# Causal attention on one core: score products in F32R on halves of the partitions, two heads at a time

## The chip, the cores and the metric

The kernel runs on one core of a Trainium2 chip. TensorE (PE) multiplies, VectorE (DVE), ScalarE (ACT) and GpSimd (POOL) work beside it, and SyncE (SP) issues most transfers. The metric is the device time of one execution in microseconds: median 2697.65 us of three runs (2695.6 to 2702.26).

## The reference, cut to what matters

Two layers, each attention times a gated mixture of experts. The change lies in the first attention and in what prepares it; x is 2 x 2048 x 256, with 16 heads of 16.

```python
xn = _layernorm(x)
q = (xn @ Wq.T).reshape(B, S, H, hd).transpose(0, 2, 1, 3)      # k and v alike
scores = einsum('bhcd,bhsd->bhcs', qi, k) * hd ** -0.5          # a block of 64 queries
scores = where(kpos[None, :] <= qpos[:, None], scores, finfo.min)
out = einsum('bhcs,bhsd->bhcd', softmax(scores), v)
s = out @ Wo.T
g = silu(experts(xn))                                           # top 1 of 8, capacity T / 8
x = x + s * g
# layer 2: windows of 128 with a look back, rotary q and k, 16 heads of 64; experts top 2 of 8
```

## The kernel before, in words

The stages follow each other: stage_project (layer norm, q, k, v, router), stage_attention, stage_experts, stage_join, stage_windows. T = 4096 rows are worked in chunks of CH = 512; P = 128, TC = 4 tiles a chunk, QC = 4 chunks a batch entry, KT = 16 key tiles.

**stage_project.** Per chunk, q and k come as four products psq[m] in PSUM. Each is written as three bf16 parts whose sum is the float32 value: ACT takes the first (L425), DVE the rest (L367), ACT the second part (L430), DVE the third (L372). SP stores all three to qk_parts in DRAM (L308). PE's next products wait for the rest (L476).

**stage_attention** goes through eight groups: four groups of GH = 4 heads (`groups`, L630), each for both batch entries u. q and k are loaded six times each, in pairs of parts, to stand on 96 partitions (parts_q, parts_k, L587), so that one bf16 matmul with 96 rows gives a product of nearly float32 precision. Three more rows of kb are ones and three of qa hold minus the query's maximum in three parts (MR = 99), so the score product comes out with the maximum subtracted.

Each group has two streams, woven by attention_steps (L493) into one list that all engines follow in order:
- "A" (maxima, a_step L715): 128 queries by up to 512 keys of one head into one of three single banks (RING = 3), DVE reduces the bank to a maximum (L859) and frees it. On the diagonal a second matmul adds -1e30 to future keys (L724). PE waits for the bank's own last user, three turns back (L720). When a chunk of queries is complete ("M"), DVE splits the negated maxima (L866 to L870), PE turns them ("MT", L731), DVE copies them out (L876) and SP writes them as rows of qa (L691).
- "S" (scores, L774): 128 keys by up to 512 queries of one head into one bank of a pair; the mask is added by a matmul on the diagonal (L777). After two heads ACT takes the exponentials of both banks (L836) into one of four slots of probs. "PV" (L792): for four heads, v with a column of ones times the probabilities, in float32, each head on its own 32 output partitions, accumulated over key tiles; it stands one key tile behind the scores. At a chunk's end "COPY" (ACT, L844) and "O" (four turns through a ring bank, L802, and the division, L906 and L909).

The A stream runs half a group ahead of the scores (LEAD = 0.5): its first half for group 0 is the head (L736), and each group carries the second half of its own maxima and the first of the next. GpSimd meanwhile fills constant parts (L655 to L660), clears expert_in (L665) and scatters 32 tiles into it (L668). SP loads the next group's q, k and v (L677 to L679) ahead of the rows of maxima that follow in its queue.

## Time and profile before

| | us |
|---|---|
| median of 3 runs | 2697.65 |
| lowest, highest | 2695.6, 2702.26 |
| span of the profiled execution, its own time from first to last instruction | 2692.8 |
| PE, DVE, ACT, POOL busy | 2451.3, 1846.2, 1406.8, 815.1 |

The profile is of one execution; no time but its span is given for it. Start and duration in the timeline are in us, the trace's PE rows are matmuls and its PEld rows weight loads. Matmuls are pipelined, so successive starts tell their rate and not their duration. The projections end at about 132 us, the first attention at 1157 us.

### The profile page before, as it was taken

Reading aid. Unit: us, or ns where it says so; the run is one execution under the profiler, and the core shown is the slowest. Engines: PE = TensorE matmul, PEld = TensorE weight load, DVE = VectorE, ACT = ScalarE, POOL = GpSimd, SP = SyncE. Lnnn points to the kernel's source line nnn. Section 1 sums busy time; section 2 is a strip of 40 time slices with the busy share of each in tenths; the row PEclk is TensorE's granted clock in tenths of the full one; section 3 lists DMA queues with packets and bytes.
Section 4 is the critical chain, followed back from the end, with each engine's and each line's share of the span. In section 5 each row is a group of like instructions: output and inputs, shape, how many; then the busy total and the mean of one; then the engine's idle time right before and its main releaser. Section 6 shows DMA issues by size and latency. Waiting matters only on the chain. (4 is left out here: it accounts for less than half of the span.)

```text
span 2692.8 us, 51134 instructions
## 1 busy us (share of the span) xinstructions
PE 2451.3 (91%) x16420; PEld 1589.0 (59%) x16420; DVE 1846.2 (69%) x3682; ACT 1406.8 (52%) x2776; POOL 815.1 (30%) x647
## 2 busy tenths in 40 slices
PE   5648999999999999969977599999999999999999
PEld 4512333333333333358866477777777777777777
DVE  7757877877787777424438476777667767766776
ACT  3404655656565566755634255555555555555554
POOL 1070000000000000014425355554455555444553
PEclk9858999999999999989988699999999999999999
DMA  4574041321404040033257000000000000000000
GB/s 135 191 170 65 5 62 26 41 52 16 61 6 62 6 60 5 7 127 133 102 177 241 18 13 12 11 13 13 13 13 13 9 11 13 13 13 13 13 9 9
DMA packets 189865, 132.85 MB, mean 49 GB/s; under 512 B 99857, under 2 KB 177687, under 8 KB 189712
## 3 DMA queue, kind: packets, MB, share of 16 engines
q1 hardware_dynamic: 160048, 100.06, 15.4%
q10 hardware_dynamic: 24160, 14.16, 2.2%
q0 software_dynamic: 5504, 16.69, 1.7%
q8 instruction: 83, 1.36, 0.2%
q14 instruction: 70, 0.57, 0.1%
HBM read 84.43 MB, written 46.14 MB: 48 GB/s over the span
## 5 line engine op out<-in xcount | busy, mean ns | idle before, releaser
L859 DVE TENSOR_REDUCE a_best<-a_ring 128x1 f32<-128x512 f32 (+3 forms) x1280 | 700.9, 604 | 214.0 <-PE a_ring L721 123.0
L836 ACT ACTIVATE a_probs<-a_pss 128x1024 f32<-128x1024 f32 (+3 forms) x640 | 554.0, 895 | 452.6 <-PE a_pss L777 228.7
L721 PE MATMUL a_ring<-a_kb,a_qa 96*128 96x512 bf16 (+3 forms) x1280 | 453.0, 365 | 67.2 <-DVE a_best L859 32.3
L774 PE MATMUL a_pss<-a_qa,a_kb 99*128 99x512 bf16 (+3 forms) x1280 | 433.9, 353 | 15.6 <-issue 7.2
L1771 ACT ACTIVATE w_probs<-w_pss,w_top 128x256 f32<-128x256 f32 x512 | 239.0, 476 | 379.7 <-DVE w_top L1859 365.0
L1606 POOL TENSOR_TENSOR w_probs<-w_probs,w_inv 128x512 f32<-128x512 f32 x256 | 301.0, 1176 | 395.7 <-DVE w_inv L1865 386.3
L962 POOL TENSOR_TENSOR e_w_r<-e_w,e_w_r 128x1024 fp32r<-128x1024 f32 x28 | 67.0, 2402 | 1032.7 <-ACT e_w_r L1035 1032.7
L1629 PE MATMUL w_psw<-wqkv,w_xr 128*128 128x512 f32 x1152 | 301.5, 398 | 11.6 <-POOL w_xr L1563 11.6
L774 PEld LDWEIGHTS a_pss<-a_qa,a_kb 99*128 99x128 bf16 x1280 | 123.5, 98 | 302.6 <-ACT a_probs L836 224.5
L792 PE MATMUL a_acc<-a_probs,a_vg 128*32 128x512 f32 (+3 forms) x2560 | 299.9, 541 | 0.1
L1669 PE MATMUL w_pss<-w_kd,w_qt 128*128 128x256 f32 x1536 | 278.4, 310 | 0.0
L1859 DVE TENSOR_REDUCE w_top<-w_pss 128x2 f32<-128x512 f32 x256 | 176.8, 691 | 141.5 <-PE w_pss L1669 140.7
L721 PEld LDWEIGHTS a_ring<-a_kb,a_qa 96*128 96x128 bf16 x1280 | 126.4, 99 | 223.9 <-DVE a_best L859 128.6
L1629 PEld LDWEIGHTS w_psw<-wqkv,w_xr 128*128 128x128 f32 x1152 | 205.6, 190 | 47.6 <-POOL w_xr L1563 12.1
L1669 PEld LDWEIGHTS w_pss<-w_kd,w_qt 128*128 128x128 f32 x1536 | 222.0, 195 | 4.1
L1629 PE MATMUL w_psw<-we,w_xr 128*128 128x512 f32 x768 | 204.2, 401 | 0.0
L1710 PE MATMUL w_pso<-w_pt,w_v 128*64 128x128 f32 x2048 | 168.3, 285 | 0.1
L1689 PE MATMUL w_pst<-identity,w_probs 128*128 128x128 f32 x1024 | 155.7, 275 | 0.0
L1629 PEld LDWEIGHTS w_psw<-we,w_xr 128*128 128x128 f32 x768 | 134.9, 188 | 22.9 <-issue 0.2
L1689 PEld LDWEIGHTS w_pst<-identity,w_probs 128*128 128x128 f32 x1024 | 123.6, 140 | 31.2 <-issue 5.7
L1882 DVE SCALAR_TENSOR_TENSOR w_y<-w_psw,coef,w_y 128x256 f32<-128x256 f32 x224 | 108.3, 484 | 42.4 <-PE w_psw L1629 23.2
L1710 PEld LDWEIGHTS w_pso<-w_pt,w_v 128*64 128x64 f32 x2048 | 106.5, 136 | 49.6 <-issue 49.1
(223 smaller groups left out, 3771.2 us busy)
## 6 DMA issues: line engine op xcount, KB each, us to landing
e_w<-in_w SPq DMA_DIRECT2D x16, 1024.0 KB, 7.9
qk_parts<-p_parts SPq DMA_DIRECT2D x32, 384.0 KB, 3.7
a_qa<-qk_parts SPq DMA_DIRECT2D x192, 64.0 KB, 2.5
a_kb<-qk_parts SPq DMA_DIRECT2D x42, 256.0 KB, 9.5
p_xin<-in_x SPq DMA_DIRECT2D x8, 512.0 KB, 5.4
v_rows<-p_vout SPq DMA_DIRECT2D x8, 512.0 KB, 5.1
a_vg<-v_rows SPq DMA_DIRECT2D x32, 128.0 KB, 9.1
expert_in<-zero POOLq DMA_DIRECT2D x16, 256.0 KB, 8.3
```

Of the source, the lines that this page charges most:

```text
L721: ins = pe.matmul(bank[:, 0:keys], qa[u][0:QR, i // TC, h, (i % TC) * P:(i % TC + 1) * P], kb[u][0:QR, h, k * CH:k * CH + keys], start=Tru ...
L774: ins = pe.matmul(pss[idx % 2][:, e, lo:CH], kb[u][0:MR, h, j * P:(j + 1) * P], qa[u][0:MR, c, h, lo:CH], start=True, stop=(j < TC * c))
L792: ins = pe.matmul(acc[32 * h:32 * h + 32, lo:CH], vg[u][:, j, h, :], probs[:, 2 * (pv % 2) + h // 2, h % 2, lo:CH], start=(j == 0), stop=( ...
L836: act.activation(probs[:, idx % 4, :, lo:CH], pss[idx % 2][:, :, lo:CH], ACT.Exp).then_inc(exp_done, 1)
L859: vec.tensor_reduce(best[:, i // TC, h * TC + i % TC, k:k + 1], bank[:, 0:keys], X, ALU.max).then_inc(ring_taken, 1)
L1606: pool.tensor_tensor(probs[:, p % 4, :, :], probs[:, p % 4, :, :], inv[:, :, p:p + 1].to_broadcast([P, 2, 2 * P]), ALU.mult).then_inc(p_re ...
L1629: ins = pe.matmul(psw[bank][:, :], xr[a][:, src, k, :], moving(b, k), start=(m == 0), stop=(m == len(pairs) - 1))
L1669: ins = pe.matmul(scores, qt[a][:, p, :], keys[b][:, p, :, :], start=False, stop=(a, b) == PARTS[-1])
L1689: ins = pe.transpose(pst[r % 2][:, 2 * e + role, :], probs[:, p % 4, e, role * P:(role + 1) * P], keep["identity"][:, :])
L1710: ins = pe.matmul(pso[e * DH:(e + 1) * DH, p % 4, :], v[(u + 1 + role) % 2][:, h * DH:(h + 1) * DH], pt[:, p % 2, 2 * e + role, :], start= ...
L1771: ins = act.activation(probs[:, p % 4, e, :], pss[p % 2][:, e, :], ACT.Exp, bias=top[:, e, p:p + 1], accum_out=rows[:, e, p:p + 1])
L1859: vec.tensor_reduce(top[:, :, p], pss[p % 2][:, :, :], X, ALU.max, negate=True).then_inc(top_ready, 1)
```

## The change: what it does

q and k are split into two F32R parts instead of three bf16 parts. The three products of parts (high-high, high-low, low-high) take 48 rows, with two rows for the maxima 50. The even head of a pair stands on partitions 0 to 49, the odd one on 64 to 113. "A" and "S" are steps of two heads: an A step fills two ring banks and waits for ring_taken up to the first item of the pair before; an S step fills both banks of a pair. The mask of the maxima becomes four bf16 matmuls of 64 rows, two for each half. The scores get no mask: the exponentials of the diagonal block are cleared by GpSimd (affine_select, behind a one-column add), and PV waits on future_cleared there. The rows of ones come by four transfers from a constant instead of a memset on GpSimd; neg_parts is split in three steps instead of five; the rows of maxima go out in four transfers of float32 instead of three of bf16. The number of q and k loads stays 24 and 6, and so do their bytes; a store of parts is 512 KB instead of 384.

```diff
-QR = 6 * HD
-MR = QR + 3
+QR = 3 * HD
+MR = QR + 2
+HALF = P // 2
...
+            for half, low_base in ((0, -HALF), (1, 0)):
+                for part, base in ((slice(0, P), low_base), (slice(0, HALF), HALF * half)):
+                    ch.link(pool.memset(keep["turn_halves"][part, half, :], 0.0))
+                    ch.link(pool.affine_select(out=keep["turn_halves"][part, half, :], in_=keep["turn_halves"][part, half, :],
+                                               compare_op=ALU.not_equal, fill=1.0, base=base, pattern=[[-1, P]],
+                                               channel_multiplier=1))
+                    ch.link(pool.affine_select(out=keep["qk_halves"][part, half, :], in_=keep["zero16"][part, :],
+                                               compare_op=ALU.is_ge, fill=NEG, base=base, pattern=[[-1, P]],
+                                               channel_multiplier=1))
+            ch.link(pool.memset(keep["ones32"][:, :], 1.0))
...
-        rest = st.sb("rest", [P, 4, CH])
-        parts = st.sb("parts", [P, 4, 3, CH], BF16)
+        parts = st.sb("parts", [P, 4, 2, CH], F32R)
...
-                def rest_of(m):
-
-                    vec.wait_ge(first_part, 4 * c + m + 1)
-                    vec.scalar_tensor_tensor(out=rest[:, m, :], in0=psq[m][:, :], scalar=HD ** -0.5 if m < 2 else 1.0,
-                                             in1=parts[:, m, 0, :], op0=ALU.mult, op1=ALU.subtract).then_inc(rest_ready, 1)
-
-                def third(m):
-                    vec.wait_ge(second_part, 4 * c + m + 1)
-                    vec.tensor_tensor(parts[:, m, 2, :], rest[:, m, :], parts[:, m, 1, :], ALU.subtract
-                                      ).then_inc(parts_ready, 1)
-
                 for m in range(4):
-                    rest_of(m)
-                for m in range(4):
-                    third(m)
+                    vec.wait_ge(high_part, 4 * c + m + 1)
+                    vec.scalar_tensor_tensor(out=parts[:, m, 1, :], in0=psq[m][:, :], scalar=HD ** -0.5 if m < 2 else 1.0,
+                                             in1=parts[:, m, 0, :].bitcast(F32), op0=ALU.mult, op1=ALU.subtract
+                                             ).then_inc(parts_ready, 1)
...
-        for h in range(GH):
+        for g in range(GH // 2):
             for i in range(TC * c, TC * c + TC):
                 for k in range(c + 1):
-                    maxima.append((h, i, k))
+                    maxima.append((g, i, k))
...
-            for h in range(GH):
-                steps.append(("S", c, j, h))
+            for g in range(GH // 2):
+                steps.append(("S", c, j, g))
...
-    parts_q, parts_k = (0, 0, 1, 1, 0, 2), (0, 1, 0, 1, 2, 0)
-    n_loads = len(parts_q) * QC + len(parts_k)
+    parts_q, parts_k = (0, 0, 1), (0, 1, 0)
+    q_loads, k_loads = 2 * len(parts_q), 2 * len(parts_k)
+    n_loads = q_loads * QC + k_loads
+    M = GH * TC
+    M_LANDED = 4 * 16
...
-        qa = [st.sb(f"qa{u}", [MR, QC, GH, CH], BF16) for u in range(2)]
-        kb = [st.sb(f"kb{u}", [MR, GH, S], BF16) for u in range(2)]
+        qa = [st.sb(f"qa{u}", [P, QC, GH // 2, CH], F32R) for u in range(2)]
+        kb = [st.sb(f"kb{u}", [P, GH // 2, S], F32R) for u in range(2)]
...
-            for u in range(2):
-                pool.memset(kb[u][QR:MR, :, :], 1.0).then_inc(ones_set, 1)
...
+            for g, i, u, order in groups(pool):
+                idx = 0
+                for s in order:
+                    if s[0] == "S":
+                        _, c, j, hp = s
+                        if j >= TC * c:
+                            lo = (j - TC * c) * P
+                            pool.wait_ge(exp_done, primed + g * n_s + idx + 1)
+                            pool.tensor_tensor(spare[:, idx % GH:idx % GH + 1], keep["zero"][:, 0:1], keep["zero"][:, 0:1], ALU.add)
+                            block_probs = probs[:, idx % GH, :, lo:lo + P]
+                            pool.affine_select(out=block_probs, in_=block_probs, compare_op=ALU.is_ge, fill=0.0, base=0,
+                                               pattern=[[0, 2], [1, P]], channel_multiplier=-1).then_inc(future_cleared, 1)
+                        idx += 1
...
+            def masked(bank, e, x, stop):
+
+                return pe.matmul(bank, keep["turn_halves"][half(e, HALF), x, :], keep["qk_halves"][half(e, HALF), x, :],
+                                 start=False, stop=stop)
+
+            def a_step(u, s, r, banks):
+                _, dg, g, i, k = s
                 keys = min(CH, (i + 1) * P - k * CH)
                 diagonal = k == i // TC
 
-                wait(pe, ring_taken, r + 1 - RING)
-                ins = pe.matmul(bank[:, 0:keys], qa[u][0:QR, i // TC, h, (i % TC) * P:(i % TC + 1) * P],
-                                kb[u][0:QR, h, k * CH:k * CH + keys], start=True, stop=not diagonal)
+                wait(pe, ring_taken, r + 2 - RING)
+                for e in range(2):
+                    ins = pe.matmul(banks[e][:, 0:keys], qa[u][half(e, QR), i // TC, g, (i % TC) * P:(i % TC + 1) * P],
+                                    kb[u][half(e, QR), g, k * CH:k * CH + keys], start=True, stop=not diagonal)
+                    if not diagonal:
+                        ins.then_inc(ring_full, 1)
                 if diagonal:
-                    ins = pe.matmul(bank[:, keys - P:keys], keep["identity16"][:, :], keep["mask_qk"][:, :],
-                                    start=False, stop=True)
-                ins.then_inc(ring_full, 1)
+                    for x in range(2):
+                        for e in range(2):
+                            ins = masked(banks[e][:, keys - P:keys], e, x, x == 1)
+                            if x == 1:
+                                ins.then_inc(ring_full, 1)
...
+            for u in range(2):
+                for e in range(2):
+                    at = HALF * e + QR
+                    sp.dma_start(kb[u][at:at + 2, :, :].bitcast(F32).rearrange("o g (k n) -> o (g k) n", n=CH),
+                                 keep["ones32"][0:2, :].unsqueeze(1).to_broadcast([2, GH // 2 * S // CH, CH])
+                                 ).then_inc(ones_set, 16)
...
-                        if e == 0:
-
-                            pe.wait_ge(exp_done, primed + g * n_s + max(idx - 1, 0))
-                        ins = pe.matmul(pss[idx % 2][:, e, lo:CH], kb[u][0:MR, h, j * P:(j + 1) * P],
-                                        qa[u][0:MR, c, h, lo:CH], start=True, stop=(j < TC * c))
-                        if j >= TC * c:
-                            ins = pe.matmul(pss[idx % 2][:, e, lo:lo + P], keep["identity16"][:, :],
-                                            keep["mask_kq"][:, :], start=False, stop=True)
-                        if e == 1:
-                            ins.then_inc(s_ready, 1)
-                            idx += 1
+                        if j == 0 and hp == 0:
+
+                            pe.wait_ge(m_landed[c], M_LANDED * (g + 1))
+
+                        pe.wait_ge(exp_done, primed + g * n_s + max(idx - 1, 0))
+                        for e in range(2):
+                            ins = pe.matmul(pss[idx % 2][:, e, lo:CH], kb[u][half(e, MR), hp, j * P:(j + 1) * P],
+                                            qa[u][half(e, MR), c, hp, lo:CH], start=True, stop=True)
+                        ins.then_inc(s_ready, 1)
+                        idx += 1
                     elif s[0] == "PV":
                         _, c, j = s
                         lo = max(0, j - TC * c) * P
-                        pe.wait_ge(exp_done, primed + g * n_s + 2 * pv + 2)
+                        if j < TC * c:
+                            pe.wait_ge(exp_done, primed + g * n_s + GH // 2 * (pv + 1))
+                        else:
+                            pe.wait_ge(future_cleared, g * n_diagonal + GH // 2 * (j + 1))
...
-                vec.wait_ge(ring_full, r + 1)
-                vec.tensor_reduce(best[:, i // TC, h * TC + i % TC, k:k + 1], bank[:, 0:keys], X, ALU.max
-                                  ).then_inc(ring_taken, 1)
+                for e in range(2):
+                    vec.wait_ge(ring_full, r + e + 1)
+                    vec.tensor_reduce(best[:, i // TC, e, g * TC + i % TC, k:k + 1], banks[e][:, 0:keys], X, ALU.max
+                                      ).then_inc(ring_taken, 1)
...
                 ch.link(vec.tensor_copy(neg_parts[:, 0, :], neg[:, :]))
-                ch.link(vec.tensor_tensor(neg_rest[:, :], neg[:, :], neg_parts[:, 0, :], ALU.subtract))
-                ch.link(vec.tensor_copy(neg_parts[:, 1, :], neg_rest[:, :]))
-                vec.tensor_tensor(neg_parts[:, 2, :], neg_rest[:, :], neg_parts[:, 1, :], ALU.subtract).then_inc(m_split, 1)
+                vec.tensor_tensor(neg_parts[:, 1, :], neg[:, :], neg_parts[:, 0, :].bitcast(F32), ALU.subtract
+                                  ).then_inc(m_split, 1)
```

In stage_project ACT's second(m) (L428) is gone too, and PE's L476 waits for parts_ready. qk_parts becomes [2, 2, D, T] in float32.

## Rows read from the trace of the kernel before

**Rows 1.** Page, part 1: busy us (share of the span) xinstructions.
```profile
PE 2451.3 (91%) x16420; PEld 1589.0 (59%) x16420; DVE 1846.2 (69%) x3682; ACT 1406.8 (52%) x2776; POOL 815.1 (30%) x647
```
**Rows 2.** Timeline, main part's first score, last division: start, us, engine, line, op.
```profile
223.60 0.63 PE L774 MATMUL a_pss<-a_qa,a_kb 99*128 99x512 bf16 x1
...
1156.40 0.42 DVE L909 TENSOR_TENSOR a_oout<-a_ring,a_inv 128x256 f32<-128x256 f32 x1
```
**Rows 3.** Windows: stretch, length, engines' busy us (instructions), PEclk, DMA share, GB/s.
```profile
43.00:55.00 12.00, 10.45 (x61) 9.00 (x60) 11.47 (x39) 7.65 (x19) 1.04 (x1) 1.00 0.72 232
151.00:183.00 32.00, 26.42 (x95) 8.74 (x95) 29.21 (x68) 0.00 (x0) 18.98 (x27) 0.50 0.79 218
185.00:214.00 29.00, 4.90 (x12) 0.89 (x10) 5.13 (x8) 0.00 (x0) 19.62 (x20) 0.50 0.30 112
280.00:320.00 40.00, 38.63 (x271) 14.63 (x263) 32.41 (x79) 23.69 (x27) 0.00 (x0) 1.00 0.03 6
```
**Rows 4.** Waits, 140 to 1100 us: us in total, times, longest.
```profile
DVE a_best L859 <- PE a_ring L721: 122.1, 170, 4.1
```
**Rows 5.** Timeline, weight loads of two PV bursts three turns apart.
```profile
265.01 0.16 PEld L792 LDWEIGHTS a_acc<-a_probs,a_vg 128*32 128x32 f32 x8 [0.43 <-issue]
...
273.68 0.16 PEld L792 LDWEIGHTS a_acc<-a_probs,a_vg 128*32 128x32 f32 x8 [0.16 <-issue]
```
**Rows 6.** Timeline, maxima, scores and one PV burst.
```profile
258.91 1.28 DVE L859 TENSOR_REDUCE a_best<-a_ring 128x1 f32<-128x512 f32 x2
...
260.24 0.10 PEld L721 LDWEIGHTS a_ring<-a_kb,a_qa 96*128 96x128 bf16 x1 [0.32 <-DVE a_best L859]
260.24 0.39 PE L721 MATMUL a_ring<-a_kb,a_qa 96*128 96x512 bf16 x1
...
260.47 0.38 PE L774 MATMUL a_pss<-a_qa,a_kb 99*128 99x512 bf16 x1
...
260.84 0.39 PE L721 MATMUL a_ring<-a_kb,a_qa 96*128 96x512 bf16 x1
261.16 0.16 PEld L792 LDWEIGHTS a_acc<-a_probs,a_vg 128*32 128x32 f32 x8 [0.23 <-issue]
...
262.16 0.10 PEld L774 LDWEIGHTS a_pss<-a_qa,a_kb 99*128 99x128 bf16 x1 [0.84 <-ACT a_probs L836]
```
**Rows 7.** F32R in the second layer: durations in ns, min/median/max, and timeline.
```profile
L1629 PEld LDWEIGHTS w_psw<-we,w_xr x5: 188/188/192, 1707.4 to 1708.2; 128*128 128x128 f32 x5
L1629 PE MATMUL w_psw<-we,w_xr x4: 393/395/478, 1707.4 to 1708.2; 128*128 128x512 f32 x4
...
1707.44 1.18 PE L1629 MATMUL w_psw<-we,w_xr 128*128 128x512 f32 x4
...
1704.52 1.55 PE L1629 MATMUL w_psw<-we,w_xr 128*128 128x512 f32 x6
```
**Rows 8.** Groups by shape, 245 to 1110 us: busy us, mean ns, idle before.
```profile
L859 DVE TENSOR_REDUCE a_best<-a_ring 128x1 f32<-128x128 f32 x115 | 32.4, 282 | 8.1 <-PE a_ring L724 8.1
```
**Rows 9.** Timeline, a group's end.
```profile
581.49 0.58 ACT L844 COPY a_sums<-a_acc 128x512 f32<-128x512 f32 x1 [0.55 <-PE a_acc L792]
...
582.20 0.65 PE L802 MATMUL a_ring<-identity,a_sums 128*128 128x128 f32 x4 [0.78 <-ACT a_sums L844]
```
**Rows 10.** GpSimd: a select at the start, a two-operand pass in the second layer.
```profile
L117 POOL TENSOR_SCALAR_AFFINE_SELECT identity<-identity 128x128 f32<-128x128 f32 x1 | 0.3, 283 | 0.2 <-POOL identity L116 0.2
...
L1606 POOL TENSOR_TENSOR w_probs<-w_probs,w_inv 128x512 f32<-128x512 f32 x256 | 301.0, 1176 | 395.7 <-DVE w_inv L1865 386.3
```
**Rows 11.** Groups of the projections, 43 to 91 us.
```profile
L425 ACT ACTIVATE p_parts<-p_psq 128x512 bf16<-128x512 f32 x17 | 10.2, 597 | 15.7 <-DMA qk_parts<-p_parts 15.7
L372 DVE TENSOR_TENSOR p_parts<-p_rest,p_parts 128x512 bf16<-128x512 f32 x16 | 10.0, 686 | 0.2 <-ACT p_parts L430 0.2
```
**Rows 12.** Timeline, GpSimd's memset of ones and SP's loads for group 1.
```profile
137.02 13.79 POOL L660 MEMSET a_kb<- 3x8192 bf16 x2
...
182.57 33.66 SPq L641 DMA_DIRECT2D a_qa<-qk_parts  x15
```

More of the change, by code:

```diff
@@ L882, in _ @@
                 if s[0] == "A":
-                    take(s, r, ring[r % RING])
+                    take(s, r, [ring[(r + e) % RING] for e in range(2)])
                 elif s[0] == "M":
@@ L894, in _ @@
                     if s[0] == "A":
-                        take(s, at, bank)
+                        take(s, at, [bank_of(u, r + e) for e in range(2)])
                     elif s[0] == "M":
```

159 lines of the change are left out of this document (82 added, 77 removed).

## The prediction

> **What bounds the kernel now.** The page first: PE is busy for 91% of the span [rows 1]. Then the windows: the change lies in the projections (before 132 us) and in the first attention, which runs from 151 to 1156 us; its main part, eight head groups, takes 932.8 us from the first score product to the last division [rows 2], 116.6 us a group. In the middle of it, at a granted clock of 1.00, PE is busy 38.6 of 40 us, DVE 32.4, ACT 23.7 [rows 3]: PE's in-order stream is the bound, with DVE's maxima close behind. The waits say how close: DVE waited 122 us for score products for the maxima [rows 4], in gaps of under a microsecond. Between bursts of the value product (PV), one turn with full widths (8 score matmuls, 4 reductions, 2 exponentials, PV) takes 2.89 us, a third of the way from the first row to the last of [rows 5]. In PE's own terms: a bf16 matmul of 512 columns follows the one before after 0.22 us, and from PV's first weight load to the next 128-column load is 1.00 us, 0.10 us after the stream before it ended [rows 6]: 8 x 0.22 + 1.00 + 0.10 = 2.86.
>
> **What the change does to PE's work.** A score product of one head (96 or 99 rows, bf16) becomes one of 48 or 50 rows in F32R on one half of the partitions; two heads go together. F32R streams 512 columns in (1.55 - 0.40)/5 = 0.23 us [rows 7], no slower than bf16. Whether two halves of rows run at once no row shows. Bounds: 0.23 us a pair if they do, 0.47 if not. I take 0.23, since PV puts four column strips side by side: eight float32 matmuls of 512 columns in 1.00 us, which one after another would need at least 8 x 0.22 [rows 6]. With it PE's stream of a full turn falls from 2.86 to 4 x 0.23 + 1.10 = 2.0 us, and PE is no longer the bound. The Trainium skill (TensorEngine Tiling, Tiling Modes) says that tiles of 64 x 128 work independently and load and multiply in parallel; by it the sum below stands, against it the rival of 2820 us holds; the trace agrees for columns, 1.00 us for eight.
>
> **What is late next: the ring of three banks.** DVE itself could do a pair of full reductions in 2 x 0.60 (two in 1.28 us, the last of them 0.68) [rows 6]. But a pair of maxima now takes two banks at once, and its matmuls wait until the first bank of the pair before is free. So the reductions form a chain: reduction 0.68; from its end to the weight load 0.05 (reductions end at 260.19, load at 260.24) [rows 6]; weight load and product L; to DVE 0.04. For bf16 L is 0.39 [rows 6]. An F32R weight load takes 188 ns against 98, and after a wait the product took 478 ns instead of 395, 0.03 us after the load's start [rows 7]: L = 0.50. Another matmul was streaming then, so L may be as little as 0.40; I take 0.50, the row's own value. Period of a full pair: 0.68 + 0.05 + 0.50 + 0.04 = 1.27 us. Narrow ones: a reduction of 128 columns takes 282 ns [rows 8], so 133 ns a step up to 512; L falls by 0.05 a step; the diagonal's mask is now two more pairs of 128 columns, 0.11 us. That makes 1.38, 1.20, 1.02 and 0.82 us for diagonal pairs of 512, 384, 256 and 128. A group has 48 full pairs and 8 of each diagonal width: 61.0 + 35.4 = 96.4 us.
>
> **What crosses this chain.** PE keeps program order: score pair, maxima pair, score pair, maxima pair, PV. Between two maxima without PV everything fits under 1.27 us. With PV in between, PE needs: load 0.11, pair 0.23, gap 0.10, PV 1.00, score load 0.11 and pair 0.23, less the 0.11 of the next load behind it: 1.67 us, 0.40 over the chain; after a narrow pair 0.53 to 0.79. A full turn becomes 1.27 + 1.67 = 2.94 us, against 2.89 now: the halved PE work is given back whole. By the order of the steps there are 26 such full-width crossings a group, 18 after full pairs and 8 after narrow ones: 18 x 0.40 + 8 x 0.61 = 12.1.
> - Single-bank turns: after one (4 of the maxima, 3 outputs inside the group) the next pair must wait for both banks of the pair before: 0.60 each after maxima, 0.65 after outputs, 4.4 in all; the maxima's split holds DVE 0.65 us, four times, 2.6. The split loses two of its five steps, which is in the 0.65.
> - Stretches with narrow scores and few maxima, where PE waits for exponentials: 1.5 + 1.0, estimated from the narrow turns of now. The group's end: after the last maxima pair its stream and two narrow PVs end at 2.6 us; the last PV waits for its exponentials and their clear, to 3.4, and takes 0.3; copy 0.6, four turns 0.65 [rows 9], a score pair: 5.4 us, 4.1 over a chain period, 0.7 of it the clear.
> Sum 96.4 + 12.1 + 7.0 + 6.6 = 122.1; about 1.5 of it coincides (splits that fall beside a PV): 120.6 us a group against 116.6, +4.0. The last group has maxima in only half: 7.5 x 4.0 = +30 us. With L = 0.40 the 52 periods without PV lose 0.10 each: 115.4, -9 us. If the two row halves load weights one after the other, 28 crossings gain up to 0.2: +5.6 a group, +42.
>
> **The clears.** 32 a group: a one-column add and a select over 128 x 256. Select over 128 elements 0.28 us, a GpSimd two-operand pass over 512 elements 1.18 [rows 10]: between 0.3 and 0.6 for 256, I take 0.45, and 0.1 for the add. GpSimd is idle in the main part [rows 3]. PV stands a whole turn (2.9 us) behind its exponentials, so 1.1 us for two is hidden, except at the group's end (counted). The mask matmuls that go from the scores (64 x 0.06 us) save PE time that no longer bounds.
>
> **Projections.** DVE is busy 11.5 of 12 us a chunk, PE 10.5 [rows 3]: DVE bounds. Four of its passes of 0.69 us go [rows 11], and ACT's four. PE and its waits are next at about 10.8. Seven chunks by 1.2: -8 us. Bounds: 0, if the stores (512 KB in place of 384 KB each; ACT already waits for them) take over, and -14.
>
> **The head of attention** (151 to 223.5 us) runs at granted clock 0.50, DVE-bound at first, then almost still from 185 to 214 (12 matmuls in 29 us, [rows 3]), while SP issues the next group's loads (182.57, 33.7 us for 15) beside the scatter. The chain at half clock costs 1.5 us for a full pair against 1.2: 43 pairs, +16 us with masks. The 13.8 us memset of ones goes from GpSimd [rows 12], so the scatter ends that much earlier and the still stretch shrinks: -12. Net +4, bounds -20 and +20. The loads keep number and bytes; four small loads of ones come behind them, covered by the head.
>
> **Sum.** The span is 2692.8 us; the median of the runs, 2697.65, is 4.9 above it, and I keep that. 2697.65 + 30 - 8 + 4 = 2724 us.
>
> **Rivals.**
> - Faster: the F32R weight load hides, so L = 0.40, and the head gives back more of its still stretch (0 net instead of +4). Then 2697.65 - 9 - 8 = 2681. It decides at L = 0.42, where the main part breaks even. For it: in steady streams F32R at 256 columns keeps pace; against it: the 478 ns row.
> - Row halves in turn: the full crossing grows by 0.47, the other periods are still the chain's: +13 a group: 2697.65 + 17 x 7.5 - 4 = 2820. Against it stand PV's strips.
> - The clears bound: at 0.6 and 0.1, a GpSimd whose spans are longer under DVE's traffic could pass 1.2 us each; eight in each diagonal are then 10 us, against some 8 us of other work there: +1.5, four times a group: 2724 + 45 = 2769. For it: GpSimd pays 1.18 us for 512 elements [rows 10].
> - The clock: with PE's stream at two thirds, it could stay at 0.50 as in the head, where PE was busy 26 of 32 us and was not granted more [rows 3]. A full turn at 1.2 GHz is some 4.8 us, 60% more: near 3280. Against it: the projections hold 1.00 at 10.5 of 12 us. The Trainium skill (TensorE: Matmul & The Clock Gate, Part 1) calls the throttled state the default that activity releases; the head agrees, 0.50 throughout.
>
> **How the numbers follow.** This kernel's runs tell 0.3% (8 us) from no change. Forecast 0.52 (its own range 2705 to 2750), faster 0.25, clears 0.10, row halves in turn 0.10, clock 0.03. The faster rival lies in part within 0.3% only if the head disappoints. Faster 0.27, same 0.15, slower 0.58. Range: 2668, below the faster rival by the projections' and head's bounds, to 2795, which takes in the clears, or the serial weight loads with the bounds of head and projections.
>
> **What would show it.** Right: in the full turns, pairs of reductions start 1.27 and 1.67 us apart in turn, DVE's idle time before them ends with a maxima matmul, PE is busy clearly less than 38 of 40 us, and the group takes 119 to 122 us. The two matmuls of a pair start within 0.02 us. Wrong: L of 0.40 in the wait-limited pairs; matmuls of a pair 0.23 apart; PV waiting for selects inside a group; a granted clock under 1 in the main part; projections no shorter than now.

## The result, and the profile after

The changed kernel took 2881.5 us, the median of 4 runs (2871.6 to 2894.9), the kernel before 2696.6 us beside it (2693.3 to 2702.3): a ratio of 1.068, 95% interval 1.065 to 1.072. Measured again on another chip it was 1.069 (1.065 to 1.073). The forecast was 2724 us, its range 2668 to 2795: slower was right, the size was not.

The page of the kernel after, part 1 (against [rows 1]), and from part 2 the granted clock of PE in 40 slices, in tenths:

```profile
PE 2495.5 (87%) x16420; PEld 1618.0 (56%) x16420; DVE 1846.4 (64%) x3591; ACT 1390.2 (48%) x2744; POOL 945.0 (33%) x1168
...
PEclk9756788786869687867998769999999999999999
```

The same row of the page of the kernel before:

```profile
PEclk9858999999999999989988699999999999999999
```

This is the first thing to see. Slices 4 to 18 hold the main part before, 4 to 19 after. Before, the clock stands at its upper level (1.00, 2.4 GHz) there; after, it goes back to 0.50 (1.2 GHz) again and again. Two windows give it as one number each: the whole main part, first score product to last division, before (its ends are in [rows 2]):

```profile
223.60:1156.80 933.20, 891.19 (x6176) 337.39 (x6174) 702.83 (x1443) 569.05 (x672) 0.00 (x0) 0.99 0.21 32
```

and windows of the kernel after: a projection chunk; the stretch in the middle of the head in which PE and DVE hardly work, called the still stretch here; the main part, and within it four of 10 us and one of 40 us:

```profile
42.00:54.00 12.00, 11.39 (x74) 10.09 (x72) 10.04 (x35) 5.95 (x18) 1.39 (x2) 1.00 0.81 276
...
172.00:203.00 31.00, 4.05 (x22) 1.94 (x22) 4.82 (x10) 0.00 (x0) 20.75 (x22) 0.50 0.22 90
...
236.80:1343.40 1106.60, 936.38 (x6130) 357.84 (x6128) 716.26 (x1380) 567.65 (x672) 138.97 (x512) 0.79 0.17 26
...
440.00:450.00 10.00, 7.92 (x66) 3.13 (x66) 7.17 (x16) 5.28 (x6) 0.00 (x0) 0.95 0.00 0
450.00:460.00 10.00, 9.42 (x53) 3.49 (x51) 4.76 (x11) 3.18 (x4) 2.19 (x8) 0.50 0.01 3
460.00:470.00 10.00, 9.37 (x61) 4.17 (x61) 5.83 (x14) 4.49 (x7) 2.19 (x8) 0.50 0.00 1
470.00:480.00 10.00, 9.09 (x54) 3.54 (x52) 6.43 (x12) 5.28 (x7) 0.00 (x0) 0.68 0.01 1
...
480.00:520.00 40.00, 31.41 (x257) 11.88 (x255) 30.00 (x58) 22.16 (x26) 4.33 (x16) 1.00 0.03 7
```

The main part grew from 933.2 to 1106.6 us. At clock 1.00 PE is busy 31.4 of 40 us, against 38.6 before [rows 3]: thinned, as forecast. In 440 to 450 us its busy time is 7.9 of 10, and then the clock is 0.50, for 27 us in this case. Over the main part there are 30 such falls with 475 us at 0.50; before there were 2 with 18 us. At 0.50 PE's busy share reads higher (9.4 of 10), because the same instructions take longer: a full engine is here a sign of a slow one.

The timeline of a full turn after, at clock 1.00, compared with [rows 5] and [rows 6]:

```profile
500.82 0.16 PEld L812 LDWEIGHTS a_acc<-a_probs,a_vg 128*32 128x32 f32 x8
500.82 1.07 PE L812 MATMUL a_acc<-a_probs,a_vg 128*32 128x512 f32 x8
...
502.58 2.57 DVE L881 TENSOR_REDUCE a_best<-a_ring 128x1 f32<-128x512 f32 x4 [0.64 <-PE a_ring L738]
503.33 0.19 PEld L738 LDWEIGHTS a_ring<-a_kb,a_qa 48*128 48x128 f32 x2 [0.99 <-DVE a_best L881]
503.33 0.50 PE L738 MATMUL a_ring<-a_kb,a_qa 48*128 48x512 f32 x2 [0.54 <-DVE a_best L881]
503.76 0.16 PEld L812 LDWEIGHTS a_acc<-a_probs,a_vg 128*32 128x32 f32 x8 [0.24 <-issue]
```

From one value product to the next 503.76 - 500.82 = 2.94 us, the forecast's number. The two maxima products of a pair, one on each half of rows, share one start and together last 0.50 us: they run side by side, and L is 0.50. DVE's four reductions stand back to back for 2.57 us, with one gap a turn that ends with the pair behind the value product: 2.94 - 2.57 = 0.37 us between full turns, 0.64 us here, where two reductions of 384 columns stood before it. A full turn at clock 0.50, same kernel:

```profile
260.65 1.93 PE L812 MATMUL a_acc<-a_probs,a_vg 128*32 128x512 f32 x8
...
262.52 0.79 PE L795 MATMUL a_pss<-a_qa,a_kb 50*128 50x512 f32 x2
...
264.52 0.80 PE L738 MATMUL a_ring<-a_kb,a_qa 48*128 48x512 f32 x2 [0.36 <-DVE a_best L881]
265.25 0.20 PEld L812 LDWEIGHTS a_acc<-a_probs,a_vg 128*32 128x32 f32 x8 [0.44 <-issue]
```

265.25 - 260.65 = 4.60 us: the value product takes 1.93 us instead of 1.07, and every full turn that falls into a stretch at 0.50 (a cold one, for short) costs 1.66 us more.

To part the clock from the rest, cut each group into its 40 turns (two exponentials each), take for each turn of the group the shortest time in seven groups, of those free of cold time where there are any, and add them: 115.9 us before, 124.1 after. That is +8.2 us, or 62 us over 7.5 groups (the last group has maxima in only half). The other 112 of the main part's 173 us are then put down to the clock.

This split is not clean, and it gives the clock too little. The 2nd, 3rd, 6th, 7th, 14th and 15th turn of a group are partly cold in all seven groups after, and they hold 4.3 of the 8.2 us; the 34 turns that are seen at full clock give 3.9. Experiment 10 below, which only adds work, has the 6th turn at full clock at 3.87 us (5.24 here) and the 14th at 3.08 (4.47 here). These two alone move 2.8 us a group to the clock: the turns are then +5.4 us a group, some 41 us, and the clock has some 132 us. A check from the other side: in the places seen at both levels, 82 cold turns are together 94 us longer than the median of the others in the same place; the 3rd, 6th, 7th, 14th and 15th turns are together, over seven groups, 43 us above their times in experiment 10. And the four executions of this kernel go with the clock: 2894.9 us with a mean of 0.869 over the span, 2871.6 with 0.879.

| us | before | after | difference | forecast |
|---|---|---|---|---|
| projections, end | 132.3 | 124.2 | -8.1 | -8 |
| loads, to the first maxima product | 18.9 | 19.6 | +0.7 | 0 |
| head | 72.4 | 93.0 | +20.6 | +4 |
| main part, sums of shortest turns | 7.5 x 115.9 | 7.5 x 124.1 | +62 (some 41 at full clock) | +30 |
| main part, the rest: the clock | | | +112 (some 132) | 0 |
| the rest of the span | 1536.0 | 1540.3 | +4 | 0 |

The waits of DVE after, 140 to 1290 us, show where its idle time went (against 122.1 us in [rows 4]), and the rows of GpSimd's clears with PE's wait for them what these cost:

```profile
DVE a_best L881 <- PE a_ring L738: 208.9, 288, 4.1
DVE a_best L881 <- PE a_ring L728: 139.8, 173, 18.0
...
PE a_acc L812 <- POOL a_probs L668: 10.5, 28, 0.6
...
L668 POOL TENSOR_SCALAR_AFFINE_SELECT a_probs<-a_probs 128x256 f32<-128x256 f32 x256 | 104.6, 409 | 0.0
L666 POOL TENSOR_TENSOR a_spare<-zero 128x1 f32<-128x1 f32 x256 | 49.8, 195 | 1002.6 <-ACT a_probs L856 1000.4
```

### The profile page after: what moved, and what is told of

Read it like the earlier page. It is cut to its first block and busy times, and to the rows that moved or that the text cites. A ratio compares the mean times of both kernels' runs of the same rounds, so it can differ in the third digit from the quotient of the medians.

```text
span 2883.7 us, 51101 instructions
## 1 busy us (share of the span) xinstructions
PE 2495.5 (87%) x16420; PEld 1618.0 (56%) x16420; DVE 1846.4 (64%) x3591; ACT 1390.2 (48%) x2744; POOL 945.0 (33%) x1168
## 5 line engine op out<-in xcount | busy, mean ns | idle before, releaser
L881 DVE TENSOR_REDUCE a_best<-a_ring 128x1 f32<-128x512 f32 (+3 forms) x1280 | 721.1, 606 | 381.9 <-PE a_ring L738 209.2
L738 PE MATMUL a_ring<-a_kb,a_qa 48*128 48x512 f32 (+3 forms) x1280 | 329.9, 512 | 221.1 <-DVE a_best L881 190.9
L812 PE MATMUL a_acc<-a_probs,a_vg 128*32 128x512 f32 (+3 forms) x2560 | 376.4, 667 | 10.6 <-POOL a_probs L668 10.5
L666 POOL TENSOR_TENSOR a_spare<-zero 128x1 f32<-128x1 f32 x256 | 49.8, 195 | 1002.6 <-ACT a_probs L856 1000.4
L738 PEld LDWEIGHTS a_ring<-a_kb,a_qa 48*128 48x128 f32 x1280 | 149.5, 230 | 362.9 <-DVE a_best L881 330.0
L795 PE MATMUL a_pss<-a_qa,a_kb 50*128 50x512 f32 (+3 forms) x1280 | 323.7, 513 | 9.4 <-issue 7.1
L795 PEld LDWEIGHTS a_pss<-a_qa,a_kb 50*128 50x128 f32 x1280 | 143.1, 225 | 324.7 <-issue 160.7
## 6 DMA issues: line engine op xcount, KB each, us to landing
expert_in<-zero POOLq DMA_DIRECT2D x16, 256.0 KB, 16.9
```

The lines of the kernel that those rows point to most:

```text
L738: ins = pe.matmul(banks[e][:, 0:keys], qa[u][half(e, QR), i // TC, g, (i % TC) * P:(i % TC + 1) * P], kb[u][half(e, QR), g, k * CH:k * CH ...
L795: ins = pe.matmul(pss[idx % 2][:, e, lo:CH], kb[u][half(e, MR), hp, j * P:(j + 1) * P], qa[u][half(e, MR), c, hp, lo:CH], start=True, stop ...
L812: ins = pe.matmul(acc[32 * h:32 * h + 32, lo:CH], vg[u][:, j, h, :], probs[:, GH // 2 * (pv % 2) + h // 2, h % 2, lo:CH], start=(j == 0), ...
L881: vec.tensor_reduce(best[:, i // TC, e, g * TC + i % TC, k:k + 1], banks[e][:, 0:keys], X, ALU.max).then_inc(ring_taken, 1)
```

## The experiments

Two theories at the start. A: PE's stream, thin after the change, is what lets the granted clock fall, and the fall is most of the loss. B: the turns are longer by their waits and the clock does little. All runs below were timed beside the kernel before; "fills" are products written into a score bank ahead of the scores that overwrite them, which change nothing in the output. The columns: ratio to the kernel before with its interval; a full turn (the 17th of a group); sum of the shortest turns, as above; the main part; time at clock 0.50 in it with the number of falls. Experiments 1 to 4 and 9 to 15 ran on chips where the kernel before takes 2670 to 2673 us, the others where it takes 2695 to 2697. The head is shorter on the former (last section), so experiments of different chips are compared by their main parts; that a main part is the same on both was not measured. All columns but the ratio are of one profiled execution; those of experiments 1 and 9 took 32 and 19 us more than their medians. In most runs two to nine of the 40 turns are partly cold in all seven groups, so differences of two or three us in the group's sum are not read.

| | ratio | full turn | group | main | cold, falls |
|---|---|---|---|---|---|
| before | 1 | 2.96 | 115.9 | 933 | 18, 2 |
| after | 1.068 (1.065 to 1.072) | 2.95 | 124.1 | 1107 | 475, 30 |
| 1 scores doubled | 1.055 (1.049 to 1.062) | 3.17 | 132.3 | 1109 | 290, 24 |
| 2 own-bank waits | 1.040 (1.036 to 1.043) | 2.93 | 119.2 | 1069 | 428, 26 |
| 3 before, pair waits | 1.032 (1.030 to 1.035) | 3.42 | 127.3 | 1015 | 19, 2 |
| 4 no clears | 1.059 (1.055 to 1.062) | 2.94 | 126.3 | 1080 | 423, 31 |
| 5 after again | 1.069 (1.065 to 1.073) | 2.93 | 125.4 | 1099 | 448, 29 |
| 6 fills on all rows | 1.075 (1.073 to 1.078) | 3.26 | 135.4 | 1132 | 166, 18 |
| 7 before, lighter | 1.025 (1.021 to 1.029) | 3.26 | 122.2 | 987 | 107, 16 |
| 8 fills at narrow turns | 1.086 (1.082 to 1.089) | 2.94 | 134.3 | 1163 | 349, 29 |
| 9 bf16 halves | 1.011 (1.008 to 1.014) | 2.74 | 116.2 | 981 | 285, 33 |
| 10 fills in the gap | 1.047 (1.043 to 1.050) | 2.93 | 125.9 | 1038 | 144, 16 |
| 11 value product cut | 1.043 (1.036 to 1.050) | 2.62 | 117.9 | 1045 | 414, 29 |
| 12 both of 2 and 11 | 1.022 (1.018 to 1.026) | 2.60 | 114.7 | 1011 | 364, 27 |
| 13 before, thin | 1.016 (1.013 to 1.020) | 3.05 | 116.8 | 971 | 154, 17 |
| 14 bf16 and both | 0.991 (0.988 to 0.995) | 2.43 | 107.3 | 908 | 171, 18 |
| 15 the same, fills | 0.998 (0.996 to 0.999) | 2.69 | 110.2 | 938 | 110, 12 |
| 16 two bf16 parts | 0.973 (0.971 to 0.975) | 2.42 | 105.9 | 880 | 160, 24 |

**1. The same work twice.**
```diff
-                        for e in range(2):
+                        for e in (0, 1, 0, 1):   # score pair
```


> The changed kernel, with each pair of score matmuls issued twice; the second overwrites the first, so the result is the same and PE has 0.23 us more to do per exponential. Theory A (the clock follows how much PE works; the chain of reductions leaves it idle and it falls to 0.50 in parts of the main part): a full turn at full clock grows from 2.94 to about 3.2 us by the crossing with PV, but the granted clock rises from 0.78 to over 0.9 in the main part, and the time falls from 2882 to about 2780. Theory B (the clock falls for another reason, such as the matmuls' 48 rows, whatever PE's load): the clock stays below 0.8 and the time rises by 60 to 100 us, to about 2960.

2828.5 us. The full turn grows by 0.22 us and the group by 8 us, as expected, or some 61 us in all; yet the main part of the profiled execution, itself 32 us over the median, is no longer than the changed kernel's, since 185 us of cold time go. A is supported, but the clock came only to 0.87 in the main part and the time is 50 us over the expectation. The four executions spread with the clock: 2860.3 us at a mean of 0.909 over the span, 2801.7 at 0.935.

**2. Each half waits for its own bank.**
```diff
-                wait(pe, ring_taken, r + 2 - RING)
                 for e in range(2):
+                    wait(pe, ring_taken, r + e + 1 - RING)
```


> The changed kernel, with each half of a maxima pair waiting for its own bank alone, so that the ring is three deep again; the halves then often run one after the other. Theory A: the chain of reductions is gone, DVE is kept at its own rate, a full turn takes about 2.6 us with PE at 2.5, the clock stays at 1.00 for nearly all of the main part, a group takes 106 to 110 us and the kernel about 2640, faster than the kernel before. Theory B: turns at full clock get shorter but the clock stays near 0.8; about 2800.

2803.7 us. The 2.6 us turn did not come: PE keeps order, and the value product still stands ahead of the next pair. The group's sum is 5 us smaller, 2.1 of them in the 6th turn, which is cold in all groups of the changed kernel and once at full clock here. The head takes 51 us where experiment 1 on the same chip has 67.

**3. The wait alone, in the kernel before.**
```diff
-                wait(pe, ring_taken, r + 1 - RING)
+                wait(pe, ring_taken, r + 2 - maxima_seen[0] % 2 - RING)
+                maxima_seen[0] += 1
```


> The kernel before (bf16, 96 rows), with one edit: every other maxima matmul waits for one bank more, as the first of a pair does in the changed kernel. Theory A: PE is now idle for lack of banks, full turns take about 3.1 us and the granted clock falls below 1.00 in the main part; the time is 2800 to 2900. Theory B: the clock stays at 1.00, and the time is about 2780 by the longer turns alone.

2759.4 us. By A the clock was to fall; it fell no more than in the kernel before, and the time is that of B. So waits for banks alone don't bring the clock down. PE was still busy 912 of 1015 us of the main part, in bf16 on all rows. What was missing for a fall is asked in 7 and 13.

**4. No clears**, and PV waits for the exponentials only (the future keys' probabilities stay in the output).
```diff
-                            block_probs = probs[:, idx % GH, :, lo:lo + P]
-                            pool.affine_select(out=block_probs, ...).then_inc(future_cleared, 1)
...
-                            pe.wait_ge(future_cleared, g * n_diagonal + GH // 2 * (j + 1))
+                            pe.wait_ge(exp_done, primed + g * n_s + GH // 2 * (pv + 1))
```


> The changed kernel without GpSimd's clears and without PV's wait for them: the probabilities of future keys in the diagonal blocks are left in, so the output is not the reference's. My prediction put 1 to 2 us a group on the clears: 10 us, 2870 against 2882. The rival that the clears bound the diagonals says 40 us or more.

2824.2 us, by its ratio 1.0% under experiment 5. Of that the main part has 19 us, and 25 us less of cold time are in it. Full turns are the same. What the clears cost stands at the group's end: its last turn at full clock takes 3.77 us, 4.64 in experiment 5, where the forecast counted 0.7 us for the clear. The sum of the shortest turns is no smaller, since nine of its turns are cold in all seven groups.

**5. The changed kernel again**, on its own chip with 6 to 8.

> The changed kernel itself, so that the experiments have it on their own chip. By its first measurement (1.068 times the kernel before, 2671 us there) about 2853 us, granted clock near 0.87 over the span. In experiment 4 the changed kernel without its clears came to 1.059 times the kernel before: if that difference is real, this one is 0.8 to 1.0% slower than it.

2878.1 us. The first measurement's ratio is confirmed. Its profiled execution is 448 us cold where the first has 475: so much the cold time varies between executions.

**6. Fills on all rows.**
```diff
+                        for t in range(4):
+                            pe.matmul(pss[idx % 2][:, 0, t * P:(t + 1) * P], keep["turn_halves"][:, 0, :],
+                                      keep["qk_halves"][:, 0, :], start=True, stop=True)
```


> Ahead of each pair of score products, at every width, PE does four bf16 products of 128 rows by 128 columns into the same bank, which the score product then overwrites: 0.24 us of work a pair, as the duplicates of experiment 1, but on all rows of the array, and also full size where the scores are narrow. Theory A (the granted clock follows PE's load): the same full turn of 3.17 us, clock 0.87 to 0.92, 2800 to 2830 us. Rival (products on half of the rows count less for the clock): clock 0.95 or more, cold time in the main part under 80 us, and about 2780 us by the longer turns.

2899.9 us, over both expectations. Clock 0.93 in the main part and cold time 166 us, between the two; it also fills narrow turns, so "on all rows" and "more of it" are not parted. The full turn of 3.26 us costs more than the clock gives back.

**7. The kernel of 3 with a thin stream.**
```diff
-                        ins = pe.matmul(pss[idx % 2][:, e, lo:CH], kb[u][0:MR, h, j * P:(j + 1) * P],
-                                        qa[u][0:MR, c, h, lo:CH], start=True, stop=(j < TC * c))
+                        ins = pe.matmul(pss[idx % 2][:, e, lo:lo + P], kb[u][0:MR, h, j * P:(j + 1) * P],
+                                        qa[u][0:MR, c, h, lo:lo + P], start=True, stop=(j < TC * c))
```


> The kernel of experiment 3 (the kernel before with the wait for a second bank at every other maxima product), and every score product cut to its first 128 columns, so that the output is not the reference's: bf16, 96 and 99 rows, no F32R in the attention. PE's stream of a full turn falls from 2.86 to about 2.2 us, in turns of 2.8 to 3.1 us: the share that the changed kernel has. Theory A (load alone): the granted clock falls to 0.8 to 0.9 over the span, with stretches at 0.50 from the groups' ends on, 2850 us. Rival (the half rows, or F32R): the clock stays at 1.00 in the main part, and the time is at or under experiment 3's 2759 us.

2760.8 us. The main part (first row: experiment 3; second: this):

```profile
209.50:1224.40 1014.90, 912.21 (x6176) 335.99 (x6174) 717.44 (x1442) 577.71 (x672) 1.96 (x2) 0.99 0.19 29
```
```profile
230.30:1216.90 986.60, 794.87 (x6180) 314.74 (x6178) 716.24 (x1442) 574.29 (x672) 0.00 (x0) 0.95 0.20 29
```

Only columns of the scores are gone (and four products write the score banks once at the start), the waits are those of 3, and the falls go from 2 to 16. So a thin stream of bf16 on all rows lets the clock fall too: A's cause is shown, in a kernel without the change. But the cold time is a quarter of the changed kernel's.

**8. Fills at narrow turns only** (eight for each score pair of fewer than 512 columns, and in the first chunk).

> The changed kernel; only ahead of score pairs narrower than 512 columns, and of all of the first chunk, PE does eight bf16 products of 128 rows by 128 columns into the two banks that the scores then overwrite (0.47 us). Full turns keep their 2.94 us and their load. Theory A with the falls set off by the thin stretches at the groups' ends and starts: falls become rare, cold time under 200 us, about 2790 us. Rival (the load of the full turns does not hold the clock, wherever the fall starts): cold time as before, 440 us or more, and 2860 us or more by the added work.

2929.7 us, the rival's side in time and in the number of falls (29), though 349 us cold are fewer than its 440. Filling the thin stretches at the groups' ends does not hold the clock, and costs 9 us a group.

**9. bf16 on row halves**: the upper 16 bits of the F32R words.
```diff
+        def tops(ap):
+            return ap.bitcast(BF16).rearrange("p (n two) -> p n two", two=2)[:, :, 1]
...
-                    ins = pe.matmul(banks[e][:, 0:keys], qa[u][...], kb[u][...], ...)
+                    ins = pe.matmul(banks[e][:, 0:keys], tops(qa[u][...]), tops(kb[u][...]), ...)
```


> The changed kernel with the maxima and score products reading only the upper 16 bits of each F32R operand, as bf16: the same halves of rows, banks, widths and order, no F32R, and less precision in the output than the change asks for. If the row halves alone make the load too light for the clock: falls and cold time as in the changed kernel (29 falls, 450 us), and only the load's part goes: L 0.50 to 0.40, non-crossing pair period 1.27 to 1.17, full turn 2.94 to 2.84, about 1.06 times the kernel before. Rival (F32R products count less than bf16 ones for the clock): clock 0.95 or more, about 1.02.

2703.7 us, where 1.06 times the kernel before was expected; the main part is 118 us shorter than experiment 5's. The turn behind a bank wait:

```profile
252.82 0.10 PEld L741 LDWEIGHTS a_ring<-a_kb,a_qa 48*128 48x128 bf16 x2 [1.07 <-DVE a_best L884]
252.82 0.40 PE L741 MATMUL a_ring<-a_kb,a_qa 48*128 48x512 bf16 x2 [0.55 <-DVE a_best L884]
253.15 0.16 PEld L815 LDWEIGHTS a_acc<-a_probs,a_vg 128*32 128x32 f32 x8 [0.23 <-ACT a_probs L859]
```

L is 0.40. The saving comes in both periods of a turn, and PE's score load behind the value product is shorter as well: 2.74 us, and 9 us a group, 69 in all. Falls are as many (33), but they are shorter, 285 us together and not 448, in an execution whose clock (0.907 over the span) is the lowest of the four (to 0.921); why is not settled.

**10. Fills in the gap**: six, ahead of the second score pair of a turn (`if hp == 1`).

> The changed kernel; ahead of the second score pair of each turn only, which stands in the period without a value product, six bf16 products of 128 rows by 128 columns go into banks that the scores then overwrite. By experiment 6 four of them cost 0.31 us where they stand on the path; this period has 1.27 us of chain over some 0.7 of PE. Expected: full turn 2.94 to 3.0 us at clock 1.00, cold time from 450 to 200 us or less, 1.04 times the kernel before. Rival (PE's added work lengthens the chain anyway): full turn 3.2, 1.07.

2792.8 us. The cleanest test of A: the full turn keeps 2.93 us, and all that changes is PE's work, in full turns in a gap. Narrow turns grow by some 0.6 us (the 11th from 1.38 to 2.02); that the sum of the turns stays at 125.9 is because turns that were always cold are now seen at full clock. Cold time goes from 448 to 144 us, and the mean clock of the span is 0.924 to 0.933 in its four executions, 0.868 to 0.879 in those of experiment 5. The main part of this and of experiment 5:

```profile
210.20:1247.70 1037.50, 963.64 (x8050) 435.43 (x8048) 716.72 (x1380) 588.17 (x672) 140.16 (x512) 0.93 0.18 28
```
```profile
234.80:1333.40 1098.60, 925.32 (x6130) 354.36 (x6128) 715.64 (x1380) 567.33 (x672) 138.78 (x512) 0.80 0.17 26
```

61 us less, with 1920 matmuls more: the clock gives back a part of the loss, shown in the changed kernel itself. The ratios, each on its own chip, say the same: 1.069 to 1.047 is 59 us. The time of 1.047 is near the expected 1.04.

**11 and 12. The value product in two column halves**, the second behind the next maxima pair; 12 has the waits of 2 as well.
```diff
+                        if 0 < j < TC * c:
+                            value(j, pv, 0, CH // 2, False)
+                            rest_of_pv = lambda ...: v(j, pv, CH // 2, CH, False).then_inc(pv_done, 1)
```


> The changed kernel with each full-width value product cut into two column halves, the second one put behind the next maxima pair, so that both periods of a turn carry half of it. By the chain theory the crossing of 1.67 us shrinks to about 1.30 and the other stays at 1.27: full turn 2.6 us at clock 1.00, PE's share 2.1 of 2.6, and with it fewer clock falls; 0.98 to 1.03 times the kernel before. Rival (the turn is not set by the crossing of bank wait and value product): 2.94 us and 1.07.

> Experiment 11 and experiment 2 together: value products in two column halves, and each half of a maxima pair waiting for its own bank. DVE's four reductions (2.4 us) and PE's stream (2.1 us) are all that is left in a full turn: 2.45 to 2.55 us at clock 1.00. With the projections' 8 us and the shorter head of experiment 2, 0.93 to 0.98 times the kernel before if the clock stays up as PE's share passes 0.8; 1.00 if it falls as often as in experiment 2.

2787.8 and 2742.4 us. The full turn is 2.5 to 2.6 us, as the chain's two periods of 1.27 foretell: the crossing of bank wait and value product was what held 2.94. Of 12's 0.93 to 0.98 nothing came: 364 us are cold.

**13. The kernel before, thinner still**: 7, and the full value product cut to 384 columns.
```diff
+                            hi = 3 * P if 0 < j < TC * c else CH
```


> Experiment 7 with each full-width value product cut to 384 of its 512 columns as well (the output is not the reference's). PE's stream of a full turn is then about 1.95 us in 2.8 to 2.9: 0.68, the share of the changed kernel (2.0 of 2.94) and of experiment 9 (1.85 of 2.74), on all rows and in bf16. If the share of PE's time alone sets the falls: about 30 falls and 250 us or more at half clock in the main part, as in experiment 9. Rival (a product on half of the rows counts less): 16 to 20 falls and 100 to 150 us, as in experiment 7.

2714.8 us, 17 falls, 154 us cold: the rival's numbers. At much the same PE time (779 us of a main part of 971; experiment 9: 782 of 981) the row halves are cold for 285 us. It speaks for half rows counting less, but masks, clears and narrow turns differ too, so it is not shown.

**14 and 15. All three together**, without and with fills in the gap.

> Experiments 9 and 12 together: products from the upper 16 bits as bf16 on row halves, a wait for each bank, the value product in two column halves. A full turn at clock 1.00 is DVE's four reductions, 2.40 to 2.50 us; sum of the turns at full clock 107 to 110 us a group against 116 in the kernel before. If the clock falls as often as in experiment 9 (285 us cold): about 0.985 times the kernel before; if the fuller stream keeps it up, 0.96.

> Experiment 14 with four bf16 products of 128 rows by 128 columns ahead of the second score pair of each turn, as in experiment 10: 0.3 us more of PE's stream a turn, which then has 2.2 of 2.45 us. Full turn 2.45 to 2.6 us, cold time half of experiment 14's or less, 0.96 to 0.98 times the kernel before. Rival (PE becomes the bound again): full turn 2.7 us and no gain over experiment 14.

2644.2 and 2663.9 us; 14 beats the kernel before by 0.9%. DVE's four reductions are now the turn: 2.43 us. The fills take 61 of the 171 us of cold time, but here they stand on PE's path (2.69 us), and cost more than they give.

**16. A version to keep**: experiment 14 with q, k and maxima written as two bf16 parts, a rounded one and its remainder.
```diff
-        parts = st.sb("parts", [P, 4, 2, CH], F32R)
-        qa = [st.sb(f"qa{u}", [P, QC, GH // 2, CH], F32R) for u in range(2)]
+        parts = st.sb("parts", [P, 4, 2, CH], BF16)
+        qa = [st.sb(f"qa{u}", [P, QC, GH // 2, CH], BF16) for u in range(2)]
...                                      # kb, neg_parts, neg_rows, qk_parts alike
```


> Experiment 14 with q, k and the maxima stored as two real bf16 parts (rounded part and remainder) in place of two F32R parts of which the upper 16 bits are read: 256 KB in place of 512 KB a chunk in the projections' stores, loads of half the bytes, operands without stride. The main part as in experiment 14: full turn 2.40 to 2.48 us, some 18 falls, 170 us at half clock. The projections are bound by DVE either way. 0.985 to 0.995 times the kernel before; under 0.985 if the strided operands or the bytes of the loads cost time.

2622.6 us, 0.973: faster than both kernels, and beyond the main expectation, in the second case that it named. Experiment 14's 12th turn of a group lasts up to 7.5 us, this one's 1.2 to 1.4: 23 us in seven groups, of the 28 by which the main part is shorter. In experiment 14 PE waits 23 us in the main part for the rows of maxima (a_qa<-a_neg_rows), seven times; here it never does. They stand in SP's queue behind loads that now have half the bytes; that the bytes are the reason was not tried by itself. Its main part, a reduction's row and the loads:

```profile
205.60:1085.70 880.10, 805.14 (x7473) 277.50 (x7472) 688.92 (x1380) 560.94 (x672) 137.93 (x512) 0.91 0.13 21
```
```profile
L894 DVE TENSOR_REDUCE a_best<-a_ring 128x1 f32<-128x512 f32 (+3 forms) x1280 | 695.7, 603 | 157.9 <-PE a_ring L738 74.4
...
a_qa<-qk_parts SPq DMA_DIRECT2D x192, 32.0 KB, 1.8
```

DVE is idle for 158 us before its reductions, 382 in the changed kernel. The projections end at 119.5 us instead of 124.2, the first maxima product starts at 130.1 instead of 143.8.

## Why the prediction was wrong

- **The step that failed** is the clock, a term that the sum puts at nothing: from "PE is no longer the bound" it took PE's spare time as free and priced every turn of the main part at 1.00. PE did go from 38.6 to 31.4 of 40 us, and the clock fell 30 times, for 475 us: 112 us of time by the sums of shortest turns, some 132 as corrected above. Experiments 7 and 10 show the cause from both sides: less work for PE brings falls to the kernel before, more work in a gap takes them from the changed one. "A granted clock under 1 in the main part" was one of the prediction's own signs of being wrong. The clock rival had the mechanism, at a chance of 0.03 and with a price for a clock that never rises (near 3280). It held as its counterweight the projections, at 1.00 with PE busy 10.5 of 12 us (0.87) [rows 3]; the main part after stands at 0.79 at clock 1.00, under the projections and even under the head's 26 of 32 (0.83), which was granted 0.50 and reads high for that reason. The rows to compare with were there. The case between, a clock that falls and returns, was not priced: 475 us at 0.50, where a full turn takes 4.6 us.
- **Full turns** were right: 2.94 us, L 0.50, both halves of rows at once; experiments 11 and 9 take away the crossing and the load, and the turn moves by what they cost. The rival of row halves in turn falls.
- **The group** was near right: 121.3 us at full clock by the corrected sum against 120.6, +5.4 us over the kernel before and not +4.0. The base of 116.6 is close to the 115.9 of the shortest turns by luck: it is an eighth of the main part, in which the last group, with half its maxima, takes 92.6 us and the seven others 119.3 on average. Which turns hold the remaining 1.4 us was not taken apart.
- **Clears**: 409 and 195 ns against 0.45 and 0.1; hidden in full turns. The last turn of a group gains 0.87 us without them (0.7 was counted), 7 us in all. Experiment 4's main part gains 19; how much of the rest is the 25 us less of cold time stays open. PE's wait for them is 10.5 us in all, and the rival of 2769 falls.
- **Projections**: -8.1 us; PE is busy 11.4 of 12 us and is next, as said.
- **Head**: the chain at half clock was sized rightly. Outside the still stretch the head takes 62.0 us instead of 43.4 for about as many DVE instructions (84 and 87): +18.6 where +16 was counted. The term that failed is the -12: the still stretch starts at 172 instead of 185 us and lasts 31 us instead of 29, though the memset is gone. Together +20.6 in place of +4. Beside it the zeros for the expert buffer land after 16.9 us instead of 8.3; that this is the cause was not tried, and experiments 1 and 4 have it too with a head of 67 us.
- **What was right by luck and what was not**: with +41 for the turns, -8 and +21 the kernel would, by an estimate from these figures, take some 2752 us at a clock of 1.00, so "slower" did not need the clock; the size did.

On the Trainium skill's rule that the throttled state is the default and activity releases it (TensorE: Matmul & The Clock Gate, Part 1): the runs agree, and say that it holds in the midst of a kernel too, 30 falls against 2. The Trainium skill's rule of independent 64 x 128 tiles (TensorEngine Tiling, Tiling Modes) agrees with the one start and 0.50 us of a pair.

## What to carry to other kernels

Where a change takes work from TensorE and leaves the time to waits, price the clock: compare its new busy share with stretches of the same trace at 1.00 and at 0.50, and count the turns at both. Work put into a gap of the stream can be worth its cost (experiment 10), and is not once it stands on the path (6, 8, 15). Check the sum of shortest turns for turns that are never seen at full clock: they hide the clock's cost in it. Where two waits cross in one period and none in the next, cut the long instruction so that each period has half of it.

## What the runs showed of the hardware

- F32R in place of bf16 costs 0.2 us in each full turn of 2.94, by weight loads of 188 ns against 98 behind waits, though the columns stream at one rate.
- Row halves of 48 and 50 rows run side by side: two products of 512 columns last 0.50 us together in F32R and 0.40 in bf16.
- The clock fell without a long pause of PE: in the 7 us before each of the 30 falls PE's longest idle time was 1.03 us, 1.2 to 3.1 us in sum.
- More work made a kernel faster: 1920 added matmuls took 61 us from the main part (experiment 10).
- The head's length goes with the chip: 92 to 93 us in the changed kernel and experiment 5, 67 in experiments 1, 4 and 10, whose edits leave the head's products alone, on chips where the kernel before takes 2671 to 2673 us. In the first, DVE's waits in 165 to 236 us have a kind that the second lacks. The kernel before has it too, 18.9 us in six waits, so it is not what the change added to the head:

```profile
DVE a_best L881 <- remote: 20.0, 6, 7.7
```
